# GpSimd normalises the rows that it scatters, and a newly tuned order for a fused MoE, recurrence and MoE kernel

## Chip, cores and metric

One core of a Trainium2 chip. The metric is the device time of one execution in microseconds (us), lower is better. It is the median of several runs; one further execution was profiled, and its own time stands beside its span.

## What is computed

x is (16, 512, 128) in float32: 16 batches, 512 time steps, 128 features, so 8192 rows ("tokens").

```python
x = x + 0.5 * ffn(layernorm(x))        # first pass
x = x + rnn(layernorm(x))
x = x + 0.5 * ffn(layernorm(x))        # second pass

# ffn: each token goes to the one expert of 8 with the largest router logit
h = square(relu(x @ expert_fc[e]))     # 128 -> 512
out = h @ expert_proj[e].T             # 512 -> 128

# rnn: 512 steps in sequence, each over all 16 batches
h_t = tanh(x_t @ Wi.T + bi + h_(t-1) @ Wh.T + bh)
```

Layer norm has no gain and no bias: (x - mean) / sqrt(var + 1e-5). The recurrence is 512 dependent steps; the two expert passes are work for many rows at once, but a row's second pass needs its state of the recurrence, and a step needs the first pass of its rows.

## The kernel before

**Units, row tiles, product tiles.** Time is cut into 16 units of 32 steps (UNIT). A unit is 4 row tiles of 128 rows (UR), so there are 64 row tiles in all (NT). To give each expert's weights whole tiles of rows, the rows are sorted by expert through DRAM: GpSimd writes each row tile to its sorted place with an indirect DMA (a "scatter"), and product tiles of 128 rows of one expert are loaded back. Sorting is done in groups of units, the "routes": FIRST gives the sizes in units of the 3 routes of the first pass, SECOND those of the second pass; MIDDLE groups the units whose layer norm before the recurrence shares one root. Partly filled tiles make 85 product tiles in the first pass and 71 in the second, 156 in all.

**A route.** For the rows of a route: the unit is transposed on TensorE ("turn", copied back by ScalarE), multiplied by the router ("logits"), VectorE finds the expert ("pick"), TensorE counts ranks with triangular products ("rank"), VectorE turns them into positions ("place") and lists of tiles ("head", "entry" in the first pass, "list" in the second). Beside it VectorE takes the statistics ("stats", `statistics`), GpSimd the power -0.5 ("root", lines 1141 and 1144), and VectorE writes the normalised rows ("norm", `normalise`, line 1238). Then GpSimd scatters the row tiles (`scatter`, L1169 in the first pass, L1164 in the second).

**A product tile** is loaded by SyncE (`load`, L1058 and L1056), transposed (`turn_x`, L1666), copied from PSUM by VectorE (L1355) or ScalarE (L1502), multiplied by fc (L1677, 8 passes), relu on VectorE (L1361), square on ScalarE (L1495), multiplied by proj (L1687, 8 passes), and scaled on VectorE (`finish`, L1371 or L1368). In the first pass the result is stored (L1064) and gathered back in row order by GpSimd (`gather`, L1183); in the second GpSimd scatters it to the output (`put`, L1189). 12 tiles fit in the ring (RING): load g waits until the put or store of tile g-12 has landed.

**The recurrence.** A step is one small matmul (`step`, L1697, 2 passes) and one tanh on ScalarE (L1466). Before a unit's first step come "add" (first pass added to x), "mstats", "mroot", "mnorm", "turn2", "xi" and "bias".

**What sets the order.** `plan` writes the whole order of all engines before the program is built. It goes in "beats": a beat has at most one product tile in its first product and the one before it in its second, so many steps as fit between their groups of four passes, and the side work that is due. The numbers in PR weigh the urgency of each job; the planner's costs are the constants in `plan`. A beat without product tiles that has steps ("alone") puts fillers between them (`keep_warm`, L1702, one call is 2 passes of 256 columns). Before any product tile, each beat has one warm-up transpose into yp (L1707).

GpSimd's own queue is `pool_order`, made by `pool_until`. Between two scatters, gathers or puts the planner sets a "rest", a memset of 128x600 that only spends time (L1152), where it reckons that the DMA queue has not drained; before the change this is done only while steps remain (`t < T`).

**SyncE's queue.** It starts with the router, then rows_in for the first units (L1012), the zeroing of the first route's DRAM (L1017), more units, the proj weights (L1081), fc (L1083), the second route's zeroing. Units 8 to 15 come after all proj weights have been transposed (the wait on s_ptr in rows_in), since they overwrite them. Near the end stands `close` (L1069), 8 DMAs that blank what lies behind the last rows of each expert; it waits for the last "list" of the last route, and in both kernels it stands between load 134 and load 135.

Product tiles are numbered from 0 in the order in which they run, and "tile 46" below is that number.

## Time and profile before

| | us |
|---|---|
| median of 3 runs | 612.68 |
| lowest, highest run | 606.79, 624.44 |
| the profiled execution, its own time | 603.88 |
| its span | 602.0 |

The span runs from the first to the last instruction; 1.88 us lie around it. In the rows, PE is TensorE's matmuls (a float32 call counts as two, one for each pass, except in transposes), PEld its weight loads, DVE is VectorE, ACT ScalarE, POOL GpSimd, SP SyncE; a q behind the name is the engine's DMA queue. PEclk is the granted clock of TensorE as a share of full speed.

### The profile page before, as it was taken

The page shows a single profiled execution, that of the slowest core. Times are in us where ns is not written, and L with a number is a line of the kernel's source. Part 1 is how long each engine was busy: PE and PEld are TensorE (multiplying, and loading weights), DVE is VectorE, ACT ScalarE, POOL GpSimd, SP SyncE. Part 2 cuts the span into 40 slices and gives each one's busy share as a digit, 9 for nine tenths or more (in the row PEclk, how much of TensorE's full clock was granted, in tenths as well). Part 3 has the DMA queues.
Part 4 walks back from the last instruction along what each step waited for, and adds up shares of the span by engine and source line. Part 5 has one row for each costly group of instructions (what it writes and reads, how often), then busy time and mean ns, then how long its engine had stood idle before and what let it go on. Part 6 is the DMA issues. An engine that isn't in the chain of part 4 may idle for free.

```text
span 602.0 us, 16237 instructions
## 1 busy us (share of the span) xinstructions
PE 551.4 (92%) x4714; PEld 533.7 (89%) x4714; DVE 412.8 (69%) x1507; ACT 315.4 (52%) x1089; POOL 423.5 (70%) x520
## 2 busy tenths in 40 slices
PE   7799798997999989999999999998999999869991
PEld 6798698897999989999999999997889999658991
DVE  5789867886667878657876774577546466665661
ACT  2133165464666546666666666654346666425660
POOL 2699497789995778978874987838849638664552
PEclk9889999998999999999999999999999999998997
DMA  5977432221222223322321532101152301435310
GB/s 184 296 273 289 109 105 81 79 78 59 78 80 69 66 82 97 93 68 63 98 81 49 132 111 77 39 27 68 45 144 76 84 20 69 139 115 151 101 37 1
DMA packets 54163, 58.89 MB, mean 98 GB/s; under 512 B 8999, under 2 KB 42034, under 8 KB 54080
## 3 DMA queue, kind: packets, MB, share of 16 engines
q1 hardware_dynamic: 44064, 36.68, 21.0%
q0 software_dynamic: 9440, 21.06, 10.8%
q8 instruction: 42, 0.69, 0.5%
q14 instruction: 41, 0.34, 0.2%
q10 hardware_dynamic: 576, 0.13, 0.1%
HBM read 27.67 MB, written 30.62 MB: 97 GB/s over the span
## 4 chain that ended last, share of the span: by engine, by line
PE 74%; DVE 11%; issue 7%; DMA 2%; SPq 1%; ACT 1%; another core or an unknown queue 1%; ACTq 0%; POOLq 0%; DVEq 0%
PE yp L1687 23%; PE hp L1677 20%; PE z L1697 11%; PE mT L1583 4%; PE lg L1627 3%; PE xTp L1666 3%; PE hp L1702 3%; DMA hsT<-in_L_attn_x_dram 2%; PE z L1647 2%; PE yp L1707 2%; DVE pay L1238 2%; DVE r_sb L1361 2%; PE hp L1616 1%; SPq L1012 1%
## 5 line engine op out<-in xcount | busy, mean ns | idle before, releaser
L1687 PE MATMUL yp<-projT,s_sb 128*128 x1248 | 198.3, 291 | 11.6 <-ACT s_sb L1495 5.9
L1677 PE MATMUL hp<-xT_sb,w_sb 128*128 128x128 f32 x1248 | 193.2, 286 | 2.0 <-DVE xT_sb L1355 1.3
L1687 PEld LDWEIGHTS yp<-projT,s_sb 128*128 128x128 f32 x1248 | 161.3, 194 | 14.6 <-issue 14.2
L1466 ACT ACTIVATE hsT<-z 128x16 f32<-128x16 f32 x512 | 93.5, 183 | 147.5 <-PE z L1697 102.7
L1677 PEld LDWEIGHTS hp<-xT_sb,w_sb 128*128 128x128 f32 x1248 | 161.7, 193 | 3.1 <-DVE xT_sb L1355 1.4
L1697 PEld LDWEIGHTS z<-hsT,wT 128*128 128x128 f32 x1024 | 154.0, 190 | 8.9 <-ACT hsT L1466 3.0
L1697 PE MATMUL z<-hsT,wT 128*128 128x16 f32 x1024 | 158.0, 230 | 1.4 <-ACT hsT L1466 1.2
L1495 ACT ACTIVATE s_sb<-r_sb 128x256 f32<-128x256 f32 (+1 forms) x252 | 115.7, 461 | 74.5 <-issue 51.8
L1361 DVE TENSOR_SCALAR r_sb<-hp 128x512 f32<-128x512 f32 x156 | 106.9, 686 | 66.6 <-PE hp L1677 55.9
L1152 POOL MEMSET idle<- 128x600 f32 x187 | 116.0, 620 | 0.2
L1189 POOL DMA_INDIRECT out_dram<-y_sb,xs_sb x71 | 70.1, 988 | 61.7 <-DVE y_sb L1368 34.9
L1486 ACT ACTIVATE w_sb<-fc_sb 128x256 f32 (+1 forms) x250 | 111.1, 463 | 2.8 <-issue 1.2
L1183 POOL DMA_INDIRECT back<-xy_dram,pos x64 | 63.2, 988 | 24.6 <-issue 15.1
L1164 POOL DMA_INDIRECT xs_dram<-pay,pos x64 | 63.2, 987 | 23.0 <-issue 11.1
L1169 POOL DMA_INDIRECT xy_dram<-pay,pos x64 | 63.0, 984 | 22.7 <-issue 10.0
L1666 PE MATMUL xTp<-ident,xs_sb 128*128 128x128 f32 x156 | 46.3, 297 | 10.3 <-DVE xT_sb L1355 8.6
L1355 DVE COPY xT_sb<-xTp 128x128 f32<-128x128 f32 x141 | 41.7, 296 | 13.4 <-PE xTp L1666 8.9
L1238 DVE TENSOR_SCALAR pay<-pay,mv,rstd 128x128 f32<-128x128 f32 x128 | 43.3, 463 | 5.0 <-POOL rstd L1144 4.9
L1371 DVE TENSOR_SCALAR y_sb<-yp 128x128 f32<-128x128 f32 x85 | 24.5, 288 | 31.8 <-PE yp L1687 21.0
L1368 DVE SCALAR_TENSOR_TENSOR y_sb<-yp,xs_sb 128x128 f32<-128x128 f32 x71 | 20.6, 290 | 35.9 <-PE yp L1687 28.5
L1144 POOL TENSOR_TENSOR rstd<-veps,half 128x4 f32<-128x4 f32 (+4 forms) x23 | 40.0, 1738 | 1.9
L1666 PEld LDWEIGHTS xTp<-ident,xs_sb 128*128 128x128 f32 x156 | 28.8, 184 | 12.7 <-issue 11.8
(132 smaller groups left out, 564.3 us busy)
## 6 DMA issues: line engine op xcount, KB each, us to landing
xs_sb<-xs_dram SPq DMA_DIRECT2D x71, 129.0 KB
xs_sb<-xy_dram SPq DMA_DIRECT2D x85, 64.0 KB
xy_dram<-y_sb SPq DMA_DIRECT2D x85, 64.0 KB
xy_dram<-zeros SPq DMA_DIRECT2D x10, 512.0 KB, 6.0
hsT<-in_L_attn_x_dram SPq DMA_DIRECT2D x16, 256.0 KB
hsT<-n_L_ffn_expert_proj_dram SPq DMA_DIRECT2D x2, 1024.0 KB
fc_sb<-in_L_ffn_expert_fc_dram SPq DMA_DIRECT2D x1, 2048.0 KB
out_dram<-y_sb,xs_sb POOLq DMA_INDIRECT x71
```

The source lines that it names most:

```text
L1152: pool.memset(idle[:, :], 0.0).then_inc(s_idle, 1)
L1164: pool.indirect_dma_start(out=xs2_dram, in_=pay[:, n, :], in_offset=None, out_offset=bass.IndirectOffsetOnAxis(ap=pos[:, 1, n:n + 1].bitca ...
L1183: pool.indirect_dma_start(out=back[:, u % BACK, j, :], out_offset=None, in_=xy1_dram[r.index], in_offset=bass.IndirectOffsetOnAxis(ap=pos[ ...
L1189: pool.indirect_dma_start(out=out.rearrange("b t d -> (b t) d"), in_=y_sb[:, g % RING, :], in_offset=None, out_offset=bass.IndirectOffsetO ...
L1361: dve.tensor_scalar(r_sb[:, g % 2, :], hp[:, g % 2, :], 0.0, None, ALU.max).then_inc(s_relu, 1)
L1466: act.activation(state(t), z_step(t), ACT.Tanh).then_inc(s_h, 1)
L1486: act.activation(w_sb[:, g % 2, half * w:(half + n) * w], fc_sb[:, bass.ds(offsets[g] + half * w, n * w)], ACT.Copy).then_inc(s_wst, n)
L1495: act.activation(s_sb[:, g % 2, half * w:(half + n) * w, :].rearrange("p c t -> p (c t)"), r_sb[:, g % 2, half * w * P:(half + n) * w * P] ...
L1666: pe.transpose(xTp[:, 0:P], xs_sb[:, g % RING, XN:XN + D], ident[:, :]).then_inc(s_tx, 1)
L1677: mm = pe.matmul(hp[:, g % 2, h * P:(h + 1) * P], w_sb[:, g % 2, h * P:(h + 1) * P], xT_sb[:, g % 2, :], start=True, stop=True)
L1687: mm = pe.matmul(yp[:, 0:D], s_sb[:, g % 2, h, :], projT[:, bass.ds(offsets[g] + h * D, D)], start=(h == 0), stop=(h == HC - 1))
L1697: pe.matmul(z_step(t), WhT, state(t - 1) if t else hsT[:, 0:B], start=False, stop=True, skip_group_check=True).then_inc(s_mm, 1)
```

## The change

Three things are changed in the code, and with them the planner's numbers.

1. **Norm on GpSimd.** The normalisation of rows that are scattered (64 row tiles in the first pass, 64 in the second) goes from VectorE to GpSimd (`normalise_row`), one row tile at a time: the norm of row tile j+1 stands ahead of the scatter of row tile j. The norm before the recurrence ("mnorm", 64 row tiles) stays on VectorE.
2. **Rests.** They are no longer confined to the time before the last step; they stand where the new pace PACE (1.75 a DMA) asks for them.
3. **Early x.** Units 1 and 3 are loaded through ScalarE's queue, ahead of its weight loads; SyncE keeps 0, 2 and 4.

```diff
-STEP = [1, 3, 1]
-MIDDLE = [1, 1, 1, 1, 1, 1, 1, 1, 1, 1, 3, 3]
-SECOND = [3, 2, 2, 3, 2, 2, 1, 1]
+STEP = [1, 2, 1]
+MIDDLE = [1, 1, 1, 2, 1, 2, 1, 1, 1, 3, 1, 1]
+SECOND = [4, 3, 1, 2, 2, 1, 1, 1, 1]
...
+PACE = 1.75
...
-PR = {'proj': -38.387, 'lat1': 30.338, 'lat2': 69.811, 'lat3': -18.484, 'last': 24.985,
...
+PR = {'proj': 89.249, 'lat1': 194.285, 'lat2': 50.001, 'lat3': -44.694, 'last': -205.813,
...
-AHEAD = [4, 5, 7]
+AHEAD = [2, 4, 5]
...
-    ROW, LAND, WINDOW = 1.27 + REST / 900, 2.2, 3.413
+    ROW, LAND, WINDOW = PACE if REST else 1.35, 2.2, 3.413
+    NORM = 0.45
...
+                if what == "root":
+                    pool_order.append(("norm", key, 0))
+                    pool_free += NORM
+                continue
+            if what == "scatter" and p[1][2] + 1 < key.J:
+                pool_order.append(("norm", key, p[1][2] + 1))
+                start += NORM
+            while REST and drained > start + PR["burst"]:
+                pool_order.append(("rest",))
+                start += REST / 1250
+            pool_order.append(p[1])
+            pool_free, drained = start + 1.27, max(drained, start) + PACE
...
-                while REST and t < T and drained > start + PR["burst"]:
-                    pool_order.insert(-1, ("rest",))
-                    start += REST / 900
-                pool_free, drained = start + 1.27, max(drained, start) + 1.85
...
+        def by_act(u):
+
+            return u < FIRST[0] and u % 2 == 1
...
+            def normalise_row(r, j):
+
+                n, w = r.n0 + j, int(r.second)
+                if j == 0:
+                    pool.wait_ge(s_root, root_no["root", r.index])
+                pool.tensor_scalar(pay[:, n, XN:XN + D], row_in(w, n), mv[:, w, n, 0:1], rstd[:, w, n:n + 1],
+                                   ALU.subtract, ALU.mult).then_inc(s_row, 1)
...
-                if j % 4 == 0:
-                    pool.wait_ge(s_norm, 4 * norm_no["norm", r.index, j // 4])
+                pool.wait_ge(s_row, row_no[r.index, j])
...
+            for u in range(min(FIRST[0], NU // 2)):
+                if by_act(u):
+                    act.dma_start(raw(u), x[:, u * UNIT:(u + 1) * UNIT, :].rearrange("b (th j) d -> th b (j d)", j=UR)
+                                  ).then_inc(s_in[u], 16)
```

All other places of the diff follow from these (the planner's terms for "norm" go, the counters for the semaphores are split). AHEAD puts unit 7's rows behind the two proj loads instead of ahead of them. The counts that move: 187 rests become 136; 128 norms go from DVE to POOL; of the 156 copies into xT_sb, 15 stood on ACT and now 54 do; 32 filler calls (L1702) become none; the warm-up calls (L1707) go from 80 to 85. The number of passes of real work on TensorE stays.

**TensorE, after step 373 of the recurrence (counted from 1).** hp<-wT,ident is the filler, z<-hsT,wT a step, hp<-xT_sb,w_sb and yp<-projT,s_sb a tile's two products (ISA rows set an address). Before:

```order
L1697 MATMUL z<-hsT,wT 128x16
L1702 MATMUL hp<-wT,ident 128x256
L1697 MATMUL z<-hsT,wT 128x16
L1702 MATMUL hp<-wT,ident 128x256
L1697 MATMUL z<-hsT,wT 128x16
L1702 MATMUL hp<-wT,ident 128x256
```

The same place now:

```order
L1690 MATMUL xTp<-ident,xs_sb 128x128
L1701 MATMUL hp<-xT_sb,w_sb 128x128 x2
L1721 MATMUL z<-hsT,wT 128x16
L1701 MATMUL hp<-xT_sb,w_sb 128x128 x2
L1721 MATMUL z<-hsT,wT 128x16
L1711 ISA
L1711 MATMUL yp<-projT,s_sb 128x128
```

Where steps had fillers between them, they have a product tile now. In the order before, 12 beats with steps have no tile in their first product, 10 of them in one run (steps 370 to 409), and 8 tiles (44 to 51) have no step beside them, between steps 96 and 97. In the new order one beat (2 steps) has no tile, and no tile between the first and the last step is without steps. So the transposes of 25 product tiles stand ahead of the first step where there were 24, and 101 beats carry steps beside a tile where 95 did. Behind the last step stand the products of tiles 125 to 155 (126 to 155 before).

**GpSimd, the first route's scatters.** veps and rstd are the root, xy_dram<-pay,pos a scatter, idle a rest. Before:

```order
L1144 TENSOR_TENSOR rstd<-veps,half 128x20
L1169 DMA xy_dram<-pay,pos 3584x128
L1152 MEMSET idle 128x600
L1169 DMA xy_dram<-pay,pos 3584x128
L1152 MEMSET idle 128x600
```

Now:

```order
L1156 TENSOR_TENSOR rstd<-veps,half 128x20
L1163 TENSOR_SCALAR pay<-hsT,mv,rstd 128x128 x2
L1188 DMA xy_dram<-pay,pos 3584x128
L1163 TENSOR_SCALAR pay<-hsT,mv,rstd 128x128
L1188 DMA xy_dram<-pay,pos 3584x128
```

A norm stands where the rest stood; 2 of the 20 scatters of this route still have a rest as well. In the new order the second route's root and the third's (20, 12 and 32 row tiles) both stand ahead of the second route's scatters.

**GpSimd, its last instructions.** out_dram<-y_sb,xs_sb is a put. Before:

```order
L1164 DMA xs_dram<-pay,pos 67456x258 x4
L1189 DMA out_dram<-y_sb,xs_sb 8192x128 x27
```

Now (the last rows of a pattern that begins with the put of tile 126):

```order
L1208 DMA out_dram<-y_sb,xs_sb 8192x128
L1172 MEMSET idle 128x600
L1208 DMA out_dram<-y_sb,xs_sb 8192x128
L1172 MEMSET idle 128x600
L1208 DMA out_dram<-y_sb,xs_sb 8192x128
```

Before, the last route's 4 scatters stand behind the put of tile 128 and 27 puts follow without a rest; now they stand behind the put of tile 125 and 30 puts follow with a rest between any two.

## Rows read from the trace of the kernel before

**Rows 1.** The page, busy time of each engine over the span.

```profile
PE 551.4 (92%) x4714; PEld 533.7 (89%) x4714; DVE 412.8 (69%) x1507; ACT 315.4 (52%) x1089; POOL 423.5 (70%) x520
```

**Rows 2.** Windows: stretch, its length, busy time (instructions), PEclk, DMA share, GB/s.

```profile
191.00:214.00 23.00, 21.85 (x195) 20.82 (x195) 18.55 (x72) 12.09 (x28) 13.94 (x16) 1.00 0.24 68
411.00:439.00 28.00, 27.29 (x196) 23.30 (x195) 17.63 (x68) 10.39 (x48) 23.56 (x28) 1.00 0.20 63
517.00:547.00 30.00, 20.84 (x153) 18.59 (x152) 16.23 (x62) 11.54 (x22) 18.95 (x20) 0.94 0.42 129
```

**Rows 3.** L1466 (tanh): duration min/median/max, first and last start, in three stretches.

```profile
L1466 ACT ACTIVATE hsT<-z x96: 164/184/186, 120.3 to 192.4; 128x16 f32<-128x16 f32 x96
L1466 ACT ACTIVATE hsT<-z x264: 163/184/187, 216.9 to 405.3; 128x16 f32<-128x16 f32 x132
L1466 ACT ACTIVATE hsT<-z x107: 162/184/186, 439.8 to 516.6; 128x16 f32<-128x16 f32 x107
```

**Rows 4.** L1666 (one transpose a tile), in three stretches.

```profile
L1666 PE MATMUL xTp<-ident,xs_sb x24: 272/273/302, 67.0 to 117.7; 128*128 128x128 f32 x24
L1666 PE MATMUL xTp<-ident,xs_sb x10: 272/300/328, 517.0 to 546.7; 128*128 128x128 f32 x10
L1666 PE MATMUL xTp<-ident,xs_sb x20: 272/272/273, 548.7 to 584.9; 128*128 128x128 f32 x20
```

**Rows 5.** Groups of instructions: the fillers of the beats alone.

```profile
L1702 PE MATMUL hp<-wT,ident 128*128 128x256 f32 x64 | 21.4, 419 | 0.0
```

**Rows 6.** GpSimd's timeline: first root and scatters, last scatter of route 0, last put.

```profile
15.76 3.58 POOL L1144 TENSOR_TENSOR rstd<-veps,half 128x20 f32<-128x20 f32 x1
24.07 1.24 POOL L1169 DMA_INDIRECT xy_dram<-pay,pos  x1 [4.73 <-DVE pos L1284]
...
49.00 0.97 POOL L1169 DMA_INDIRECT xy_dram<-pay,pos  x1 [0.17 <-issue]
...
57.83 0.97 POOL L1169 DMA_INDIRECT xy_dram<-pay,pos  x1 [0.17 <-issue]
...
592.08 0.97 POOL L1189 DMA_INDIRECT out_dram<-y_sb,xs_sb  x1 [1.23 <-issue]
```

**Rows 7.** GpSimd's groups by form.

```profile
L1144 POOL TENSOR_TENSOR rstd<-veps,half 128x8 f32<-128x8 f32 x4 | 6.9, 1716 | 0.3
L1141 POOL TENSOR_SCALAR veps<-mv 128x4 f32<-128x4 f32 x12 | 2.9, 239 | 9.6 <-DVE mv L1232 9.5
L1141 POOL TENSOR_SCALAR veps<-mv 128x32 f32<-128x32 f32 x1 | 0.3, 312 | 0.0
L1119 POOL TENSOR_SCALAR_AFFINE_SELECT ident<-ident 128x128 f32<-128x128 f32 x1 | 0.3, 294 | 0.2 <-POOL kio_i L1117 0.2
```

**Rows 8.** VectorE and GpSimd at 46 us.

```profile
46.48 0.61 POOL L1152 MEMSET idle<- 128x600 f32 x1
46.55 0.57 DVE L1270 TENSOR_SCALAR full<-base 128x8 int32<-128x8 f32 x1
```

**Rows 9.** TensorE and VectorE at the first product tiles.

```profile
66.97 0.27 PE L1666 MATMUL xTp<-ident,xs_sb 128*128 128x128 f32 x1
69.73 0.30 PE L1666 MATMUL xTp<-ident,xs_sb 128*128 128x128 f32 x1 [2.49 <-DVE xT_sb L1355]
67.20 2.19 DVE L1238 TENSOR_SCALAR pay<-hsT,mv,rstd 128x128 f32<-128x128 f32 x8
```

**Rows 10.** SyncE's queue and VectorE behind the last step.

```profile
533.76 9.62 SPq L1069 DMA_DIRECT2D xs_dram<-blank  x8
543.91 2.33 SPq L1056 DMA_DIRECT2D xs_sb<-xs_dram  x3
533.14 0.16 DVE L1331 TENSOR_SCALAR rest_i<-total 128x8 int32<-128x8 f32 x1
528.45 1.30 DVE L1238 TENSOR_SCALAR pay<-pay,mv,rstd 128x128 f32<-128x128 f32 x4
```

**Rows 11.** VectorE's statistics of unit 3.

```profile
12.27 0.87 DVE L1228 BATCH_NORM_STATS2 stats<-hsT 128x6 f32<-128x128 f32 x4 [0.46 <-DMA hsT<-in_L_attn_x_dram]
```

81 lines of the change are left out of this document (40 added, 41 removed).

## The prediction

> **What bounds the kernel now.** I read the page's busy times first, then a table of windows, then where steps and tiles fall, then the waits of the stretches that are slow. TensorE is busy 551.4 of 602.0 us and no other engine over 424 [rows 1], so the time is TensorE's list of instructions plus its idle time, and the question is what in that list is no work. The reader is to see three regimes. Until 67.0 us no product tile runs. Between the steps' ends, 120.3 to 516.6, the recurrence is the chain: 512 steps. Outside it tiles run alone, at (584.9 - 548.7) / 19 = 1.905 us each when nothing waits [rows 4].
>
> Within the recurrence a step costs (405.3 - 216.9) / 263 = 0.716 us where tiles stand beside it, and (192.4 - 120.3) / 95 = 0.759 in the first stretch, (516.6 - 439.8) / 106 = 0.725 in the last [rows 3]. In the stretch without tiles, 411 to 439 us, TensorE looks 97% busy, but 21.4 us of such work in the whole run are fillers [rows 2, 5]: here the scan went on at its own pace and no product was made. And from 192.4 to 216.9 us no step ran at all [rows 3], while TensorE did tiles [rows 2]. Tiles and steps, which hide each other elsewhere, are apart in both places. After the last step 30 us go to ten tiles, TensorE 20.8 us busy [rows 2, 4].
>
> **The change part by part.** The sum is made against the profiled execution (span 602.0, own time 603.9), section by section.
>
> *To the first tile: 67.0 becomes 63.5.* Before, the first scatter began at 24.07, when VectorE had the positions; it had written eight norms ahead of them, and 20 scatters took until 57.83, (57.83 - 24.07) / 19 = 1.78 each [rows 6]. The norms' place on VectorE goes to GpSimd, which idled 4.73 us there, so the first scatter comes about 2.2 us earlier (eight norms took 2.19 [rows 9]). The ACT queue brings units 1 and 3 by a second queue. VectorE waited only 0.46 us for unit 3 [rows 11], and about as much for each of the others, so at most 2 us are to be had; I take 0.5. From then on the pace decides. A norm takes the place of a rest: period 0.97 + 0.17 + d, where d is the norm on GpSimd. No row has this operation (128 columns, two scalars from memory). Below: an affine select of 128 columns, 0.294 us. Above: a tensor-tensor power over 8 columns, 1.72 us [rows 7]. Nearest is the tensor-scalar of the root: 0.239 at 4 columns and 0.312 at 32, so 2.6 ns a column, 0.56 at 128 [rows 7]. I take 0.55, period 1.69, against 1.74 to 1.78 with a rest of 0.61 [rows 6, 8]; the two rests that stay cost 1.2, which eats the gain of 1 us. Scatter 20 ends near 55, and tile 0 comes 2.7 us earlier, if TensorE's own queue lets it: tile 0 started at 66.97 without a wait in front of it, behind ranks and warm-ups. The new order has the first transpose directly behind the third route's rank, with about ten beats' warm-ups fewer between. Together 3.5, between 0 and 7: proj, fc and row unit 7 change places on SyncE, and that may give back part.
>
> *Tile 0 to the first step: 53.3 becomes 49.1.* 24 transposes at 1.905 are 45.7; the other 7.6 were stalls. The first of them is plain: tile 1 waited 2.49 us for a copy that stood behind eight norms of 2.19 on VectorE [rows 9]. All norms of this stretch leave VectorE, and the copies go to ScalarE. New: 25 x 1.905 = 47.6, and 1.5 for the transposes and products of unit 0 in the last beats. First step near 112.6 instead of 120.3. The gathers that this needs stand behind the second route's scatters, 12 x 1.69 + 2.5 for rests, and two roots (the third route's stands ahead of them now, 5.8 us); from 55 that ends near 87, and tile 10, which the first gather needs, is stored near 88. Cover is small but there.
>
> *The recurrence: 396.3 becomes 368.* First to last tanh, 120.3 to 516.6. Of that 24.5 lie in the hole from 192.4 to 216.9, 23.8 over a step. The new order has no such hole; its 102 beats carry all steps, 5.0 a beat, and the stretch of 0.716 carried about the same (264 steps beside some 51 tiles). 512 steps at 0.716 are 367, at before's mean without the hole, 372.5 / 511 = 0.729, they are 373. I take 368. The eight tiles of the hole and the places of the twelve beats alone are exchanged: tiles move beside steps that had fillers. The fillers' 21.4 us [rows 5] are the same gain seen on TensorE, not a second one.
>
> *What hides this:* product tiles must be ready. Tile 46 is the first of the third route, whose 32 scatters must have landed. By rows: gathers of unit 4 wait for tile 26 and are issued until about 137; then 25 scatters at 1.69 (42), a root (1.5) and rests (1.2) give 182, landing and load 5 more, 187. TensorE gets there after 112.6 + 114 x 0.72 = 195, less at most 4 for the first beats' faster steps: 191. Cover 4 us, gone if d is 0.16 larger.
>
> *Behind the last step: 85.4 becomes 83.5.* Before: last step 516.6, the last route's list at 533.14, close until 543.4, load 135 at 543.9, tile 135 at 546.7, then 20 tiles at 1.905, end 602.0 [rows 4, 10]. The chain stays: close still stands ahead of load 135. One tile more (125) fits into the 9 us in which TensorE idled. Four norms of 1.30 us leave VectorE in this chain [rows 10]; I take 1.9. *Rests:* the scatters of the last route end 22 us behind the last step, and behind them 30 puts now follow at 0.97 + 0.61 + 0.17 = 1.75, the last starting at 22 + 29 x 1.75 = 72.8; the last put started at 592.08 - 516.6 = 75.5 before [rows 6]. So they are covered by 2.7 us, and each 0.1 us on that pace costs 2.9.
>
> *Sum.* 63.5 + 49.1 + 368 + 83.5 = 564.1 us of span, 37.9 less; with 1.9 around it 566.0. The profiled execution lies 2.9 below the lowest run and 8.8 below the median. I add the middle, 6: 572 us.
>
> *The port between VectorE and GpSimd.* VectorE's tensor-scalar over 8 columns at 46.55 took 0.57 us and ended at 47.12, 0.03 behind GpSimd's memset [rows 8]. The Trainium skill (SBUF — State Buffer, Terms) says that the two engines arbitrate for one port pair that is "exclusive, held for the full instruction"; by that rule the trace agrees. The same rule speaks against the change: a norm on GpSimd reads memory, and would be held up by VectorE in turn. That is the second case below, priced from rows.
>
> **The rivals.**
>
> *GpSimd's norms are slow, d = 0.85.* Each waits for a VectorE instruction of some 0.3 us. For it: rows 8 shows the two holding each other. Against: VectorE has 128 such writes fewer, and GpSimd 51 memsets. Period 1.99: the third route's rows are 25 x 0.3 = 7.5 later, 4 covered, 3.5 lost; the next route's 16 rows lose 5 more, with "mroot" of unit 8 behind them, later routes about 4, and the start 20 x 0.3 = 6 less 3.5 that TensorE's queue covers. 572 + 15 = 587. The Trainium skill (GPSIMD Engine Reference, section 8) calls VectorE "structurally ~2× faster" for elementwise work; twice the 0.27 us that a norm takes [rows 9] would be 0.55, by estimate, so by that alone nothing changes.
>
> *GpSimd becomes the bound: slower.* d = 1.7, as the power over 8 columns [rows 7]. Its busy time becomes 423.5 - 51 x 0.61 + 128 x 1.7 = 610, over the whole forecast. First pass: 20 + 25 scatters at 2.84 are 50 us later than forecast, 8 covered, the second pass's routes about 16 more: 572 + 58 = 630. It decides from d = 1.5. Against: no GpSimd tensor-scalar is over 0.32.
>
> *The order does not hold: no change.* The plan puts tiles beside steps that on the chip are not ready, the first steps again take 0.759 as at 120 to 192, and stalls of the hole's kind come back in small pieces. First step at 118, 512 x 0.759 = 389, then 85: 592 of span, 594, and 600 by the same 6. For it: the old plan also meant to have no stall at tiles 0 to 23. Against: what stalled those, norms on VectorE, is what leaves.
>
> *The early load is no gain.* If the two queues bring nothing and unit 7 delays the second route, 3 us go: 575, inside the first case.
>
> **How the numbers follow.** Forecast 0.70 (its own range 560 to 584), slow norms 0.12, no change 0.12, GpSimd as the bound 0.06. Within 2%, about what a measurement of this kernel can tell from no change, is 600.4 to 624.9. The forecast and slow norms lie below: faster 0.82. No change holds 0.12, GpSimd as the bound is slower, 0.06. Range 557 to 600: the low end is the forecast with the start's 7 us in full, 0.716 a step throughout, and a small offset; the high end reaches the third case.
>
> **What would show it.** First tile at 63 to 64 us, first tanh at 112 to 114, none of L1702, first to last tanh 365 to 373, last tanh to end 83 to 85. GpSimd's norms at 0.5 to 0.6 us; VectorE's busy time down by 128 norms, near 412.8 - 128 x 0.27 = 378, GpSimd's at 423.5 - 51 x 0.61 + 128 x 0.55 = 463. It is wrong if tile 46, or a unit's first step, has GpSimd's scatters or root as its releaser, or if the last put waits for puts rather than for a y.

## The result: 2 per cent slower, and the profile after

The changed kernel takes 621.27 us (median of 20 runs, 611.59 to 633.6), the kernel before 612.84 beside it (20 runs, 601.14 to 624.44): a ratio of 1.020, 95% interval 1.015 to 1.025. The forecast was 572 us, faster. The profiled execution took 619.27 us, span 617.5. Some executions of every kernel are a few per cent longer than its others, some of the profiled ones among them, so verdicts rest on ratios to the kernel before on the same chip without those runs (each with its 95% interval), and a trace is read only for durations, orders and waits.

The page of the changed kernel, busy time and the first two lines of the chain that ended last, answering to [rows 1]:

```profile
PE 554.1 (90%) x4661; PEld 544.3 (88%) x4661; DVE 379.6 (61%) x1376; ACT 324.5 (53%) x1140; POOL 507.8 (82%) x599
...
POOL 43%; PE 34%; issue 10%; DVE 7%; DMA 2%; SPq 0%; POOLq 0%; ACT 0%; DVEq 0%
POOL pay L1163 12%; PE yp L1711 9%; PE hp L1701 9%; POOL xy_dram L1188 9%; POOL xs_dram L1183 8%; PE z L1721 6%; POOL out_dram L1208 5%; POOL idle L1172 5%; POOL rstd L1156 3%; PE mT L1607 2%; PE lg L1651 2%; POOL back L1202 2%; PE xTp L1690 1%; PE z L1671 1%; PE yp L1731 1%
```

VectorE's busy time fell as forecast (378, measured 379.6), and TensorE has the instructions forecast for it, without the fillers. But GpSimd is busy for 507.8 us, not 463, and it heads the chain: 43%, with the first pass's new norms (L1163) its largest line. TensorE's list is shorter by 53 matmuls and still takes longer than before, 554.1 against 551.4.

The first reason stands in the norm's and the scatter's own rows (one line's instructions: duration min/median/max, first and last start):

```profile
L1163 POOL TENSOR_SCALAR pay<-hsT,mv,rstd x64: 792/798/998, 18.1 to 214.4; 128x128 f32<-128x128 f32 x64
L1188 POOL DMA_INDIRECT xy_dram<-pay,pos x64: 978/1064/1516, 30.6 to 217.3; - x64
```

A norm takes 0.80 us, not 0.55, and the scatter behind it 1.06, not 0.97. Even the shortest of these 64 norms took 0.792, so this looks like its duration and not like a wait for VectorE; experiment 2 confirms it. GpSimd's timeline at the first route and at its end, answering to [rows 6]:

```profile
30.55 1.24 POOL L1188 DMA_INDIRECT xy_dram<-pay,pos  x1 [10.85 <-DVE pos L1304]
31.85 0.80 POOL L1163 TENSOR_SCALAR pay<-hsT,mv,rstd 128x128 f32<-128x128 f32 x1
32.82 1.05 POOL L1188 DMA_INDIRECT xy_dram<-pay,pos  x1 [0.18 <-POOL pay L1163]
...
71.39 0.98 POOL L1188 DMA_INDIRECT xy_dram<-pay,pos  x1 [0.17 <-issue]
```

Twenty scatters stand (71.39 - 30.55) / 19 = 2.15 us apart, against 1.78 before and 1.69 in the forecast. The windows of the four sections (stretch, its length, busy time of each engine with instructions, PEclk, DMA share, GB/s), answering to [rows 2]:

```profile
0.00:76.00 76.00, 63.17 (x464) 61.89 (x464) 49.74 (x268) 17.02 (x29) 49.42 (x72) 0.96 0.60 200
76.00:134.00 58.00, 50.67 (x413) 49.72 (x414) 29.41 (x72) 32.48 (x72) 52.51 (x57) 0.91 0.39 109
134.00:524.00 390.00, 373.29 (x3223) 367.27 (x3222) 260.70 (x932) 231.39 (x943) 329.86 (x380) 0.96 0.26 76
524.00:617.00 93.00, 67.01 (x566) 65.44 (x564) 39.79 (x105) 43.60 (x97) 75.99 (x93) 0.88 0.29 83
```

By sections, forecast and measured: to the first tile 63.5 and 76.1; from there to the first step 49.1 and 58.3; first to last step 368 and 390.0; behind it 83.5 and 93.1. All four are late. GpSimd was busy for 52.5 of the 58 us of the second section: it has no slack there to catch up with.

How a late GpSimd reaches the end shows in two places. In the recurrence, VectorE's norms of a middle unit waited 4.73 us for GpSimd's root, which stood in GpSimd's queue behind a row of norms and scatters, and TensorE waited for them:

```profile
199.42 1.26 DVE L1258 TENSOR_SCALAR pay<-pay,mv,rstd 128x128 f32<-128x128 f32 x4 [4.73 <-POOL rstd L1156]
```

```profile
200.74 1.11 PE L1607 MATMUL mT<-ident,pay 128*128 128x128 f32 x4 [3.40 <-DVE pay L1258]
```

TensorE's granted clock was 0.50 from 200.7 to 208.9 us, right behind this wait, which is the lower of its two levels (1.2 GHz), and the two passes of a step took 0.45 us there instead of 0.29. So a wait costs more than its own length.

Behind the last step it is the puts that are late. VectorE had the last route's statistics at 531.95 us and its positions at 536.98, but GpSimd, working off its queue without a gap of more than 0.2 us, came to this route's root only at 543.45, and to its four scatters from 548.26 on:

```profile
543.94 1.09 POOL L1156 TENSOR_TENSOR rstd<-veps,half 128x4 f32<-128x4 f32 x1
...
548.26 1.05 POOL L1183 DMA_INDIRECT xs_dram<-pay,pos  x1 [0.17 <-issue]
...
554.29 0.98 POOL L1183 DMA_INDIRECT xs_dram<-pay,pos  x1 [0.17 <-issue]
```

The last of them started 29.8 us behind the last step; in the kernel before it was 21.5. The 30 puts that end the program stand behind it.

TensorE's longest wait of this stretch has another cause. The tile that began at 553.03 is tile 135, whose load stands behind `close`, as before. SyncE's queue and TensorE's:

```profile
541.30 0.33 SPq L1067 DMA_DIRECT2D xs_sb<-xs_dram  x1
542.12 7.03 SPq L1080 DMA_DIRECT2D xs_dram<-blank  x8
549.96 0.36 SPq L1067 DMA_DIRECT2D xs_sb<-xs_dram  x1
```

```profile
553.03 0.47 PE L1690 MATMUL xTp<-ident,xs_sb 128*128 128x128 f32 x1 [5.53 <-DMA xs_sb<-xs_dram]
553.30 1.91 PE L1701 MATMUL hp<-xT_sb,w_sb 128*128 128x128 f32 x8
...
559.30 1.06 PE L1701 MATMUL hp<-xT_sb,w_sb 128*128 128x128 f32 x8
```

By the code, load 134 (541.30) waits for the put of tile 122, whose place in the ring it takes; GpSimd issued that put at 538.88, behind the scatters of the route before the last, for which load 134 waits too. Then come the eight DMAs of `close`, and load 135. Tile 135 began 28.6 us behind the last step, where it had been 30.1, so this wait is not what the change lost. It shows the cost of the lower level once more: the granted clock was 0.50 from 553.0 to 557.9 and 1.00 behind, and from 553.03 to 559.19 two tiles took 6.2 us instead of 3.8.

### The profile page after: what moved, and what is told of

Read it like the earlier page. It is cut to its first block, busy times and chain, and to the rows that moved or that the text cites. A ratio compares the mean times of both kernels' runs of the same rounds, so it can differ in the third digit from the quotient of the medians.

```text
span 617.5 us, 16141 instructions
## 1 busy us (share of the span) xinstructions
PE 554.1 (90%) x4661; PEld 544.3 (88%) x4661; DVE 379.6 (61%) x1376; ACT 324.5 (53%) x1140; POOL 507.8 (82%) x599
## 4 chain that ended last, share of the span: by engine, by line
POOL 43%; PE 34%; issue 10%; DVE 7%; DMA 2%; SPq 0%; POOLq 0%; ACT 0%; DVEq 0%
POOL pay L1163 12%; PE yp L1711 9%; PE hp L1701 9%; POOL xy_dram L1188 9%; POOL xs_dram L1183 8%; PE z L1721 6%; POOL out_dram L1208 5%; POOL idle L1172 5%; POOL rstd L1156 3%; PE mT L1607 2%; PE lg L1651 2%; POOL back L1202 2%; PE xTp L1690 1%; PE z L1671 1%; PE yp L1731 1%
## 5 line engine op out<-in xcount | busy, mean ns | idle before, releaser
L1711 PE MATMUL yp<-projT,s_sb 128*128 x1248 | 202.9, 295 | 9.0 <-ACT s_sb L1519 8.2
L1701 PE MATMUL hp<-xT_sb,w_sb 128*128 128x128 f32 x1248 | 200.2, 292 | 0.3
L1711 PEld LDWEIGHTS yp<-projT,s_sb 128*128 128x128 f32 x1248 | 165.4, 197 | 10.1 <-issue 9.9
L1701 PEld LDWEIGHTS hp<-xT_sb,w_sb 128*128 128x128 f32 x1248 | 169.3, 201 | 1.3 <-issue 0.6
L1188 POOL DMA_INDIRECT xy_dram<-pay,pos x64 | 68.6, 1072 | 21.8 <-DVE pos L1304 10.9
L1183 POOL DMA_INDIRECT xs_dram<-pay,pos x64 | 67.8, 1060 | 20.5 <-DVE pos L1304 9.5
L1172 POOL MEMSET idle<- 128x600 f32 x136 | 84.3, 620 | 0.3
L1163 POOL TENSOR_SCALAR pay<-hsT,mv,rstd 128x128 f32<-128x128 f32 x64 | 52.3, 817 | 3.5
L1163 POOL TENSOR_SCALAR pay<-pay,mv,rstd 128x128 f32<-128x128 f32 x64 | 51.7, 807 | 3.8
L1690 PEld LDWEIGHTS xTp<-ident,xs_sb 128*128 128x128 f32 x156 | 30.1, 193 | 21.7 <-issue 12.4
L1156 POOL TENSOR_TENSOR rstd<-veps,half 128x4 f32<-128x4 f32 (+5 forms) x24 | 40.4, 1682 | 2.0
```

Source lines behind the costliest of these rows:

```text
L1163: pool.tensor_scalar(pay[:, n, XN:XN + D], row_in(w, n), mv[:, w, n, 0:1], rstd[:, w, n:n + 1], ALU.subtract, ALU.mult).then_inc(s_row, 1)
L1172: pool.memset(idle[:, :], 0.0).then_inc(s_idle, 1)
L1183: pool.indirect_dma_start(out=xs2_dram, in_=pay[:, n, :], in_offset=None, out_offset=bass.IndirectOffsetOnAxis(ap=pos[:, 1, n:n + 1].bitca ...
L1188: pool.indirect_dma_start(out=xy1_dram[r.index], in_=pay[:, n, XN:XN + D], in_offset=None, out_offset=bass.IndirectOffsetOnAxis(ap=pos[:, ...
L1701: mm = pe.matmul(hp[:, g % 2, h * P:(h + 1) * P], w_sb[:, g % 2, h * P:(h + 1) * P], xT_sb[:, g % 2, :], start=True, stop=True)
L1711: mm = pe.matmul(yp[:, 0:D], s_sb[:, g % 2, h, :], projT[:, bass.ds(offsets[g] + h * D, D)], start=(h == 0), stop=(h == HC - 1))
```

## The experiments

Each experiment but one takes the changed kernel or the kernel before and changes what its heading names; the cuts of code show the lines that matter, and "..." marks what is left out. "Period" is the mean distance of the first route's 20 scatters.

**1. The price of the norm dialled.** Two kernels keep every engine's order and replace the norm by memsets. One line gives the edit (the second has 600 for 270):

```diff
-                pool.tensor_scalar(pay[:, n, XN:XN + D], row_in(w, n), mv[:, w, n, 0:1], rstd[:, w, n:n + 1],
-                                   ALU.subtract, ALU.mult).then_inc(s_row, 1)
+                pool.memset(pay[:, n, XN:XN + D], 0.0).then_inc(s_row, 1)
+                rest(270)
...
```

> The order of the changed kernel, with GpSimd's norm in front of a scatter replaced by two memsets, 128x128 on the payload and 128x270 on an idle tile (left out: the normalising of the routed rows, which are zero here), by the memsets of before some 0.2 + 0.3 = 0.5 us against the 0.80 of the norm. Theory 'price' (the norm costs 0.80 and its scatter 1.06, so a scatter comes every 2.1 us where the plan has 1.72): period 1.6 to 1.7, last scatter of the first route near 60, first tanh at 120 to 125, no hole at the third route's first tile, time 580 to 595. Rival 'plan' (the order itself does not hold, whatever the norm takes): 610 to 621, with the same stalls. Rival 'start' (TensorE's low clock until 31 us costs the lost 6 us there and nothing else does): positions again at 30 us, 610.

Measured: 0.950 of before (0.943 to 0.956), which is 568 us beside this run's before of 598, faster than all three theories called for. GpSimd's timeline of this run:

```profile
34.61 1.04 POOL L1188 DMA_INDIRECT xy_dram<-pay,pos  x1 [0.17 <-issue]
35.65 0.23 POOL L1163 MEMSET pay<- 128x128 f32 x1
35.79 0.34 POOL L1172 MEMSET idle<- 128x270 f32 x1
36.30 0.96 POOL L1188 DMA_INDIRECT xy_dram<-pay,pos  x1 [0.17 <-issue]
```

The period is 1.68 us. And the windows of the four sections:

```profile
0.00:65.00 65.00, 55.10 (x456) 53.65 (x456) 48.39 (x268) 17.00 (x29) 44.30 (x94) 0.95 0.74 251
65.00:116.00 51.00, 47.74 (x424) 46.79 (x422) 28.63 (x72) 32.27 (x72) 43.33 (x72) 1.00 0.37 103
116.00:485.00 369.00, 359.95 (x3232) 355.45 (x3232) 258.56 (x933) 230.93 (x945) 304.27 (x478) 1.00 0.28 83
485.00:566.00 81.00, 65.43 (x558) 63.96 (x556) 38.68 (x104) 42.81 (x95) 63.79 (x86) 0.92 0.29 84
```

First tile 65.2 (forecast 63.5), first step 51.4 later (49.1), the recurrence 368.0 (368), the rest 81.9 (83.5): a span of 566.5 against 564.1. So the sections come out close to the prediction's sum once the norm's place is short. That isn't proof of every term. Scatters without a further pause stand 1.61 apart here and not 1.69, so the two memsets stand for a norm of 0.47 us rather than 0.55, 10 us less on GpSimd over 128 scatters. And the kernel before took 598 us beside this run, where it took 612.84 beside the changed kernel: as a share of before the forecast is 0.934 (572 of 612.68) and this run 0.950. What the run does show is that the new order gains 5 per cent when GpSimd's work between scatters is short. Rivals "plan" and "start" fall.

> As the run before, with 128x128 and 128x600, some 0.2 + 0.6 = 0.8 us: the norm's duration without its reads and without its scalars (left out: the normalising of the routed rows). Theory 'price', if it is the duration alone: scatter period 1.95 to 2.1, time 612 to 622, as the changed kernel. Rival 'port' (what hurts is that the norm reads memory and holds VectorE and the scatter's descriptors back): scatters 0.97 instead of 1.06, VectorE's busy time lower than 379.6, time 600 or less.

Measured: 0.996 (0.987 to 1.006), scatters 0.97 us, period 1.94. So 0.26 us more at each of 128 scatters, 33 us on GpSimd, cost 0.047 of 598 us, 28 us (the intervals leave 7 either way): most of it reaches the end. The duration alone explains two thirds of the way from 0.950 to 1.020. The remaining 0.024, 14 us (6 either way), belongs to what a real norm has and a memset has not: the scatter behind it is 0.09 longer and the period 2.15 instead of 1.94. Both theories had a part right. The first called for 612 to 622 from the duration alone, the second for 600 or less, which came, with scatters of 0.97; but the second also called for a VectorE busy for less than 379.6 us, and it was busy for 389.0. Zero data are no reason for the gain: this run has them too, and its mean granted clock lay between 0.92 and 0.97, around the changed kernel's 0.946.

**2. The norm's price by itself.** One operation after the other on GpSimd, nothing beside it but a stream of VectorE's tensor-scalars in the row "beside".

> Not the kernel: one operation after the other on GpSimd with nothing beside it (left out: everything else; the output holds rows that mean nothing), to read the price of a norm. Theory 'two scalars from memory' (the extra over the root's 0.239 and 0.312 at 4 and 32 columns comes from the per-partition scalars): 128 columns with two such scalars 0.80, with two constants 0.55. Theory 'slope' (each column costs more than the root's two widths show): constants cost the same as scalars from memory, 64 columns 0.5, 256 columns 1.3 to 1.4. Theory 'port': beside a stream of VectorE's tensor-scalars each norm is over 0.80 by what they hold it, 0.1 or more. The scatter behind a norm: 1.06 against 0.97 behind a memset if reading what GpSimd has just computed is what lengthens it.

The page's groups (line, engine, operation, out<-in, count | busy us, mean ns):

```profile
L97 POOL TENSOR_SCALAR two<-rows,mean 128x128 f32<-128x128 f32 x4 | 3.1, 784 | 8.9 <-ACT by_act L84 8.9
...
L115 POOL TENSOR_SCALAR beside<-rows,mean 128x128 f32<-128x128 f32 x8 | 6.7, 846 | 0.0
L99 POOL TENSOR_SCALAR wide<-rows,mean 128x256 f32<-128x256 f32 x3 | 3.6, 1209 | 0.0
...
L103 POOL TENSOR_SCALAR fixed<-rows 128x128 f32<-128x128 f32 x4 | 2.5, 632 | 0.0
L105 POOL TENSOR_SCALAR one<-rows,mean 128x128 f32<-128x128 f32 x4 | 2.3, 596 | 0.0
L101 POOL TENSOR_SCALAR narrow<-rows,mean 128x64 f32<-128x64 f32 x4 | 2.2, 569 | 0.0
L107 POOL TENSOR_SCALAR single<-rows 128x128 f32<-128x128 f32 x4 | 2.0, 517 | 0.0
```

One operation with a constant costs 0.517 at 128 columns ("single"); a second operation makes it 0.632 ("fixed"); two scalars from memory instead of constants 0.784 ("two"). At 64 and 256 columns the norm takes 0.569 and 1.209: 3.3 ns a column on a base of 0.36. "Beside" VectorE's stream of tensor-scalars each norm takes 0.846, 0.06 more, and VectorE's go from 0.343 to 0.403, not blocked for an instruction's length. The scatters behind a norm took 1.06 to 1.07 and behind a memset 0.97. The theory of the two scalars is right in direction: they make 0.15 of the difference. It put 0.55 on two constants, which took 0.632; the port costs 0.06, not 0.1.

**3. The mechanism in the old order.** The kernel before, VectorE's norms of routed rows moved to GpSimd and the pauses beside them dropped:

```diff
+    for w in pool_order:
+        if w[0] == "scatter":
+            while made[-1] == ("rest",):
+                made.pop()
+            if w[2] + 1 < w[1].J:
+                made.append(("norm", w[1], w[2] + 1))
+        made.append(w)
...
```

> The kernel before, its order unchanged on every other engine, with VectorE's norms of routed rows moved to GpSimd, one between two scatters, and the pauses in front of those scatters dropped: the mechanism alone, everything computed. Theory 'price' (a scatter every 2.1 us against 1.75): first route's last scatter 6 to 7 us later, the third route's rows later too, time 615 to 635, 1.02 to 1.04 of before. Rival 'order' (the changed kernel's order is what loses, the mechanism is harmless): 595 to 605 beside a before of 598, ratio within 1 per cent.

Measured: 1.015 (1.007 to 1.022), period 2.10. The mechanism costs 1.5 per cent in the old order as well, a little less than the 2 to 4 of theory "price"; the rival is out. With the mechanism the two orders are within 0.5 per cent of each other.

**4. The norms back on VectorE, in the new order.** Four a beat, behind the beat in which the plan has the root (the first route's all in the beat of its "place"); on GpSimd a pause of 600 columns, of 470, or nothing stands where the norm stood (the last has `or 0` in this line):

```diff
+            beats[k].dve.append(("norm", r, i))
...
+    pool_order = [w if w[0] != "norm" else ("rest",) for w in pool_order if w[0] != "norm" or 1]
```

> The order of the changed kernel with the norms back on VectorE, four at a time behind the beat in which the plan has the root, and a rest of 600 columns on GpSimd where the norm stood; everything is computed. Theory 'price': period 0.97 + 0.61 + 0.17 = 1.75, and 128 norms of 0.27 = 35 us back on VectorE, which waits little outside the start: 585 to 600. Rival 'plan': 612 to 622. Rival 'VectorE' (its norms delay copies and the recurrence as in the kernel before): stalls at tile 0 to 3 again, 600 to 612.

Measured: 1.009 (1.001 to 1.017), period 1.81. That is the rival "VectorE", a little more than "price" allowed.

> The same with every pause on GpSimd 470 columns wide instead of 600, so that a scatter comes every 1.6 us, as in the run with two short memsets. Against that run only VectorE's 128 norms are added. Theory 'price': 580 to 590. Rival 'VectorE': 598 to 608.

Measured: 0.984 (0.978 to 0.990), period 1.69; with all pauses narrower by 130 columns the order turns from 1 per cent slower than before to 1.6 faster. The expectation's two ranges don't decide it: as a share of the 598 us that they were made beside it is 588, "price", in its own us it is 602, "VectorE". Against the run with two short memsets, which has the same period, VectorE's 128 norms cost 0.034 or more: more, because that run still has 600 columns in the pauses beside gathers and puts.

> The changed order with the norms on VectorE and nothing on GpSimd in their place: scatters 1.1 to 1.2 us apart. Theory 'price': with GpSimd no bound, 575 to 590. Rival 'transfers' (without a pause between scatters the queue of their transfers fills, landings stay 1.6 us apart or block other loads): scatters get longer than 0.97 or land later, 590 to 605. Rival 'VectorE' (its norms cost what the run with pauses showed, whatever GpSimd's pace): 600 to 608.

Measured: 1.161 (1.153 to 1.169). All three expectations fell by far. The scatters stayed 0.97 long. Its chain of waits has a large entry that is 1% in the kernel before and absent in the changed one:

```profile
PE 69%; another core or an unknown queue 11%; DVE 9%; issue 4%; POOL 3%; ACT 2%; POOLq 0%; ACTq 0%; DVEq 0%
```

**5. Is it the missing pause or VectorE?** The norm replaced by the 128x128 memset alone:

```diff
+                pool.memset(pay[:, n, XN:XN + D], 0.0).then_inc(s_row, 1)
```

> The changed kernel with the norm replaced by the 128x128 memset alone (left out: the normalising of the routed rows), a scatter every 1.35 to 1.5 us, VectorE free. If the run with VectorE's norms and no pause (1.16) collapsed because scatters follow each other too closely: slower than the run with 0.5 us between (0.950), 0.98 to 1.15, with ScalarE's and VectorE's waits without a releaser. If it collapsed because of VectorE's norms: 0.93 to 0.95.

Measured: 1.169 (1.159 to 1.179). VectorE's norms are not needed for the loss; the missing pause is enough. ScalarE's timeline, and TensorE's beside it:

```profile
187.28 0.18 ACT L1489 ACTIVATE hsT<-z 128x16 f32<-128x16 f32 x1 [2.39 <-remote]
187.36 0.71 ACT L1518 ACTIVATE s_sb<-r_sb 128x256 f32<-128x256 f32 x2
193.07 0.18 ACT L1489 ACTIVATE hsT<-z 128x16 f32<-128x16 f32 x1 [4.99 <-remote]
```

```profile
187.52 0.61 PE L1720 MATMUL z<-hsT,wT 128*128 128x16 f32 x2 [1.16 <-issue]
187.97 1.09 PE L1606 MATMUL mT<-ident,pay 128*128 128x128 f32 x4
193.30 0.61 PE L1720 MATMUL z<-hsT,wT 128*128 128x16 f32 x2 [4.24 <-ACT hsT L1489]
```

The two matmuls of this step began at 187.52, and its tanh only at 193.07. "Remote" is a wait whose releaser the trace doesn't have. In the meantime GpSimd issued scatters 1.36 us apart, and the tanh ran 0.6 us behind the end of its next pause (191.85 to 192.46). Such waits add up to 132 us on ScalarE and VectorE here and to 12 in the kernel before (four sums of 4.0, 3.6, 3.4 and 1.1), and there are none in the changed kernel. The 12 us all lie between 520 and 543 us, behind the last step, where the kernel before has no pauses and GpSimd issues most transfers 1.27 to 1.30 us apart. But close transfers don't always bring them: the same stretch of the old kernel with 470-column pauses has transfers 1.27 to 1.36 apart and no such wait. What holds the two engines up isn't shown; that it comes with scatters 1.3 to 1.4 us apart while steps run, in both kernels without the pause, is.

**6. Pauses and tail.** All pauses of the changed kernel 470 columns wide; no pauses behind the last step; and the old kernel with 470:

```diff
-                pool.memset(idle[:, :], 0.0).then_inc(s_idle, 1)
+                pool.memset(idle[:, 0:470], 0.0).then_inc(s_idle, 1)
```

> The changed kernel with its 136 pauses 470 columns wide instead of 600; the norms stay on GpSimd. It only touches gathers and puts. Theory 'price' (the scatters' 2.1 us decides, pauses matter little): 1.00 to 1.02 of before, as the changed kernel or a little less; the tail 2 to 4 us shorter. Rival 'pause' (the narrower pause alone is what made the run with VectorE's norms and 470 columns 2.5 per cent faster than the one with 600): 0.995 or less.

Measured: 0.989 (0.980 to 0.997), the rival "pause". 136 pauses narrower by 0.11 us are 15 us less on GpSimd and gain 0.031, 19 us. That is more than one for one as the best value (the intervals leave 6 us either way), and it fits an engine that heads the chain and lifts TensorE's clock when it is early. This run's chain has GpSimd at 28% instead of 43%, and TensorE's 4661 matmuls took 543.9 us instead of 554.1.

> The kernel before with its pauses 470 columns wide instead of 600, nothing else. If the pause's width is what gained 3 per cent in the changed kernel (1.020 to 0.989), because GpSimd is its bound: here, where GpSimd is not the bound (chain of before: POOL is no large share), less, 0.985 to 1.00. If a narrower pause helps any order alike: 0.97. If the old width was needed for what the pauses guard (ScalarE and VectorE held up with no releaser in the trace, 12 us in before, 140 us in the run without pauses): 1.00 to 1.02.

Measured: 0.990 (0.986 to 0.994): a third of that gain where GpSimd isn't the bound.

> The changed kernel without GpSimd's rests behind the last step. Theory 'tail rests' (puts at 1.75 apart queue behind the last route's scatters, so that the last put, not the last y, ends the program): last tanh to end 93.1 becomes 86 to 88, time 614 to 616. Rival 'the pause is repaid in the transfers' (puts without pauses land later each, the queue fills): 619 to 622, puts longer than 0.97 us.

Measured: 1.013 (1.006 to 1.019), last tanh to end 84.8 instead of 93.1 in its profile. The direction is that of "tail rests", but the two intervals overlap, so 0.7 per cent is the best value and not a proven one.

**7. Which half of the norms.** As pause_470, with one pass's 64 norms on VectorE and pauses in their place:

```diff
+    pool_order = [("rest",) if w[0] == "norm" and not w[1].second else w for w in pool_order]
```

> As pause_470, with the first pass's 64 norms on VectorE and a 470-column pause in their place, the second pass's on GpSimd. Theory 'price' with its main cost in the first pass (20 scatters ahead of the first product tile, 32 ahead of the third route): first tanh 4 to 7 us earlier than the changed kernel's in an undisturbed run, ratio 0.985 to 0.995. If the cost sits in the second pass: 1.005 to 1.02.

Measured: 0.981 (0.973 to 0.988), a little better than expected.

> The other half: second pass's 64 norms on VectorE with a pause in their place, first pass's on GpSimd. Theory 'price' with its main cost in the first pass: 1.00 to 1.01. If the second pass's cost (tail, and gathers held up behind its scatters during the recurrence) is the larger: 0.985 to 0.995.

Measured: 1.000 (0.993 to 1.007). Against 0.989 the first pass's norms on VectorE gain 0.008 and the second pass's lose 0.012; either alone lies within the intervals, their difference of 0.020 doesn't. So moving the first pass's norms back is worth more than moving the second's. That the second's are better left on GpSimd isn't shown.

> As split_first (0.9805) with every pause 400 columns instead of 470: a scatter of the first pass every 1.57 us instead of 1.69. If GpSimd's period is still the bound: 0.965 to 0.975. If the pause has reached what it guards: 0.985 or more, with waits that have no releaser in the trace coming back.

Measured: 0.985 (0.980 to 0.990), the medians 589.6 and 603.1 us. No gain over 470 columns that can be measured, and no waits without a releaser: the pause is neither the bound nor too short here. The three kernels at 0.981 to 0.985 (first pass's norms on VectorE at either pause, all of them on VectorE at 470) can't be told apart; they compute everything, and all three beat the kernel before and the changed one.

**8. The early load.** All early units of x by SyncE's queue again:

```diff
-            return u < FIRST[0] and u % 2 == 1
+            return False
```

> The changed kernel with all early units of x on SyncE's queue again. If ScalarE's queue gains what the first root showed (14.04 us against 15.39): the first root at 15.4, first scatter 1 us later, ratio 1.02 to 1.025. If it gains nothing: first root at 14.0 and 1.02. If it is what put TensorE at its low level until 31 us in the changed kernel's profile: positions at 22 to 23 us in every run and 1.01.

Measured: 1.017 (1.008 to 1.026), GpSimd's first root operation at 14.27 us (14.04 with the two queues). It gains nothing that can be measured. The 15.39 of before was no fixed mark either: with only its pauses changed, the old kernel's root began more than 1 us earlier.

**9. The order planned anew.** The norm on GpSimd priced at 0.86 with weights searched for it, and the planner of before with 470-column pauses and weights searched for those:

```diff
-    NORM = 0.45
+    NORM = 0.86
...
```

> The norms on GpSimd as in the changed kernel, pauses of 470 columns, and the order planned anew with the norm at 0.86 us (its 0.80 and the scatter's extra 0.09) instead of 0.45, with weights searched for that price. If the loss came from a plan that believed in a cheap norm (dates slip, TensorE idles and its clock drops): 0.965 to 0.98, better than pause_470's 0.989, and fewer stretches below full clock. If the norm's time on GpSimd itself is the loss, whatever the plan: 0.985 to 1.01.

Measured: 1.027 (1.020 to 1.035), outside both expectations. The searched weights change besides the price, so this says only that this plan, made with the right price, is no better: it is worse than pause_470 by 0.038. Its chain has TensorE at 71% and GpSimd at 4%, so this order hardly waits for GpSimd any more; where its time went instead was not traced.

> The norms on VectorE as before, the planner of before with the price of 470-column pauses and weights searched for it: what a new order is worth without the moved norms. If the order is what the changed kernel had right and the norms what it had wrong: 0.96 to 0.98, no hole without steps near 192 us. If the searched order is no better on the chip than the old one: as old_pause_470 within 1 per cent.

Measured: 0.989 (0.983 to 0.994), as old_pause_470. It has no hole, and its recurrence takes 369.8 us in the profile against 395.1 in old_pause_470's; its first step comes 25.7 us later, of which 9.4 stand already at the first scatter.

**10. The norms on ScalarE.** An activation with a bias and a scale per row, two rows a beat:

```diff
+                    act.activation(pay[:, n, XN:XN + D], row_in(w, n), ACT.Identity, bias=away[:, w, n:n + 1],
+                                   scale=rstd[:, w, n:n + 1]).then_inc(s_row, 1)
...
```

> The changed order with the routed rows' norms on ScalarE (an activation with scale and bias per row, two rows a beat; the bias from one small VectorE operation a route), pauses of 470 columns on GpSimd in their place; everything computed. GpSimd's period is that of the run with two short memsets (1.65 to 1.7), and VectorE is free of the norms. If the 3.5 per cent between that run (0.950) and the run with VectorE's norms (0.984) is VectorE's load: 0.95 to 0.97. If any engine in the recurrence's chain pays as much for 128 norms (ScalarE does every tanh): 0.98 to 1.00.

Measured: 1.011 (1.001 to 1.022), worse than both expectations, with ScalarE's busy time up from 324.5 to 369.0 and 6% of the chain. No engine takes the 128 norms for nothing. With pauses of 470 columns everywhere the three homes give 0.984 (VectorE), 0.989 (GpSimd) and 1.011 (ScalarE), where the run in which nobody does them, with 600 columns beside gathers and puts, is at 0.950.

## Why the prediction was wrong, step by step

**The step that failed** is the size of d in "To the first tile": "so 2.6 ns a column, 0.56 at 128", and 0.55 taken. The slope was read from the root's tensor-scalar [rows 7], one operation with a constant. For that form it was not far off: 0.517 at 128 columns. But the norm has two operations and two scalars from memory, 0.784, and 0.80 in the kernel. The forms differed in what they do, not only in width, and the extrapolation named only the width. The bounds around it, 0.29 and 1.72, held.

**A second term was missing.** The period was put together as 0.97 + 0.17 + d, with the scatter's 0.97 from [rows 6]. Behind a tensor-scalar the scatter takes 1.06 and the whole period is 2.13 to 2.15, 0.45 above forecast, of which d is 0.25 and the scatter 0.09; the rest are gaps between them.

**The price of a slow norm was mis-sized.** The rival "GpSimd's norms are slow, d = 0.85" had the size of d right, and with 0.12 too little of the chance. That was luck: its reason, a wait for an instruction of VectorE, makes 0.06 us, and the rest is the norm's own duration. It came to 587 and not 621, because of each delay only what exceeded a cover was counted: 15 us of 128 x 0.30 = 38. The dial shows 28 of 33 us passing through, and with the real norm 42 of 60 (0.070 of 598, for 128 x 0.47). Two things stand behind this, the first read from the traces and not tested by itself. The first 20 scatters alone are 8.7 us late, more than the covers (4 us at tile 46, 2.7 at the last put), after which GpSimd's later work is late with them: third route's last scatter at 217.3 instead of the forecast 182, and 186.5 in the run with two short memsets. And waits of TensorE cost once more through its clock: its 4661 matmuls took 528.2 us with two short memsets, 554.1 here, 625.9 in the run without pauses, at mean granted clocks of 0.983, 0.946 and 0.839. The point from which GpSimd "decides" was set at d = 1.5; at d = 0.80 it is already the largest part of the chain, 43% beside TensorE's 34%.

**To the first tile**, 63.5 forecast, 76.1 measured. The prediction had the first scatter 2.7 us earlier than 24.07; where the start was not late it came at 22.9 to 24.9, at most about 1 us earlier. The period makes 19 x 0.46 = 8.7 of the lateness, of which TensorE's own queue covers some: with 470-column pauses, where the first scatter began at 23.2, tile 0 came at 69.0, 5.5 late. The other 7 us come from the start of this execution: its first scatter began at 30.55, where most with the same start have 23 to 25. TensorE's eight logit matmuls at that place, in the changed kernel and, in the next fence, in the one with 470-column pauses:

```profile
13.30 1.71 PE L1651 MATMUL lg<-wT,xrt 128*128 128x8 f32 x8
```

```profile
13.89 0.96 PE L1651 MATMUL lg<-wT,xrt 128*128 128x8 f32 x8
```

By such durations TensorE stayed at its lower level until about 28.5 us here and rose before 12 there. The first scatter is late in this way in 5 of the 14 profiles whose first route is the changed kernel's. Up to there these 14 have the same order on TensorE, so it is put down to the execution and not to the change; that one program shows both isn't shown. It doesn't make the 2 per cent: split_first's profile has it too, at 0.981. "Early load: no gain" was the right rival.

**Tile 0 to the first step**, 49.1 against 58.3: "Cover is small but there" was wrong with a period of 2.15. With 1.68 it took 51.4, so the rest of this step was right to 2.3 us.

**The recurrence**, 368 against 390.0. "The new order has no such hole" is right: no step is missing for longer than 5 us. With the cheap norm it took 368.0; that it hits the term to the tenth is luck, as the shares of before show. Between these two runs' recurrences lie 21 us by the windows: for the same steps and tiles TensorE was busy 13.3 us longer (373.3 against 360.0) and idle 8 longer. So the larger part is its clock, 0.96 against 1.00, and the waits in front of it are at least in part for GpSimd, as the 4.73 and 3.40 us at 200 us show.

**Behind the last step**, 83.5 against 93.1. The cover of 2.7 us over the last put was named as what would go, "each 0.1 us on that pace costs 2.9". The chain that the prediction followed, list, `close`, load 135, came nearly as forecast: tile 135 began 1.5 us earlier than before, where 1.9 was taken. But the last route's scatters ended 31 us behind the last step, not 22, and the puts stood behind them, 1.76 apart:

```profile
605.35 0.98 POOL L1208 DMA_INDIRECT out_dram<-y_sb,xs_sb  x1 [0.16 <-issue]
606.33 0.61 POOL L1172 MEMSET idle<- 128x600 f32 x1
607.10 0.98 POOL L1208 DMA_INDIRECT out_dram<-y_sb,xs_sb  x1 [0.17 <-issue]
```

The last put starts 82.7 behind the last step (forecast 72.8), behind a pause and not behind a y, 7 us after TensorE's last matmul. That was the sign named for "wrong".

**The port.** The prediction weighed a rule of the Trainium skill (SBUF — State Buffer, Terms) by which the two engines' port pair is "exclusive, held for the full instruction". For the norm that does not come out: with a stream on each engine both got 0.06 us longer, and the norm's shortest time in the kernel is its time alone. Beside the pauses it does, as in [rows 8]. The same small tensor-scalar of VectorE took 0.17 us once and 0.61 where a pause ran, and ended 0.02 behind it:

```profile
520.03 0.17 DVE L1353 TENSOR_SCALAR full<-rounded 128x8 int32<-128x8 int32 x1
538.13 0.61 DVE L1353 TENSOR_SCALAR full<-rounded 128x8 int32<-128x8 int32 x1
```

```profile
538.10 0.62 POOL L1172 MEMSET idle<- 128x600 f32 x1
```

In the changed kernel's trace 13 of VectorE's instructions that took over 0.1 us longer than the shortest of their form end within 0.06 us of a pause's end, and none ends so with a norm. So the full block exists in this kernel, and isn't what made the norm slow.

The other statement of the Trainium skill (GPSIMD Engine Reference, section 8), VectorE about twice as fast, would have given 0.55 and confirmed the wrong number: the norms in groups of four and eight took 0.27 to 0.33 each on VectorE and 0.80 on GpSimd, 2.4 to 3 times.

**The rivals.** "The order does not hold" is out: it holds at a period of 1.68. "GpSimd becomes the bound: slower" is what came in direction, at half the price of a norm that it was given.

What stays open: what a wait without a releaser is; why the scatter behind a tensor-scalar takes 0.09 us longer; and how a plan with the norm on GpSimd could use the order's gain, since the one searched for the right price didn't. Nor was any experiment run on the last route's root, which stood 11 us in GpSimd's queue.

## What to carry to other kernels

Price an operation from a row with the same form, its number of operations and the kind of its scalars, before its width; where there is none, the forecast isn't one number but the value at each end carried through the sum. Where an engine's work is moved onto another that issues the transfers, its period is the quantity to forecast: here most of its lateness went through to the end once the first cover was used up, and waits cost once more through TensorE's clock. A short dial run that keeps the order and replaces the operation by a memset of the forecast length tells a wrong price from a wrong plan at once.

## What the runs showed of the hardware that was not expected

- Scatters issued 1.3 to 1.4 us apart, in a kernel with 128 scatters, 64 gathers and 71 puts, came with 16 to 17 per cent more time than before, and with waits of up to 6.3 us for a tanh and 8.2 on VectorE that have no releaser in the trace. At 1.63 to 1.81 apart the profiles show none but one of 7.3 us with the norms on ScalarE, ahead of the first step, and the 12 us behind the last step of the kernel before, where its transfers stand 1.3 apart. With the norms on VectorE and pauses of 470 columns (0.51 us) the kernel took 0.984 of before, and without pauses at the scatters (600 columns elsewhere) 1.161; 600 columns (0.62) instead of 470 cost 1 to 3 per cent.
- A scatter issued behind a tensor-scalar of its own engine took 1.06 us, behind a memset 0.97, in the kernel and by itself.
- A small tensor-scalar or copy of VectorE that meets a memset of GpSimd can be held until the memset's end: 0.61 us instead of 0.17. Beside norms on GpSimd that was not seen.
- The level at which TensorE starts differs between executions whose instructions are the same up to there: eight matmuls of 8 columns took 1.71 or 0.96 us at the same place, and the profile's clock column reads 1.00 for both stretches. The matmuls' own durations tell it.
